# Attention scores on row quarters of the array, ACT and POOL in DVE's place, and a third buffer of expert products

## What is computed

```python
# 1: context-query attention (softmax over the context's tokens, then one linear layer of 4*128)
# 2: 8 experts, the best 2 weigh (weights from a softmax of two logits); all 8 are computed:
for e in range(8):
    u = x @ W1[e]; v = x @ W2[e]          # 128 -> 256
    y = (u * sigmoid(u) * v) @ W3[e]      # 256 -> 128
    out = out + y * weights[..., e]
# 3: cross attention, 16 heads of 8 features
scores = einsum('bqhd,bkhd->bhqk', Q, K) / sqrt(8)
attn = softmax(scores); out = einsum('bhqk,bkhd->bqhd', attn, V) @ W_o + b_o
# 4: x rounded to fp8, times an fp8 matrix, rescaled, plus bias
```

## Time and profile before

| | us |
|---|---|
| median of 3 runs | 224.56 (223.74 to 224.80) |
| the profiled execution | 223.94 |
| its span, first to last instruction | 222.0 |
| mean granted clock | 0.954 |
| experts (48 to 105) | 57.0 |
| change of stage (105 to 126.3) | 21.3 |
| batch 0 of the attention (126.3 to 147.2) | 20.9 |
| groups 4 to 11, nearly all in the loop (147.2 to 184.5) | 37.3 |
| groups 12 to 14 (184.5 to 197.6) | 13.1 |

### The profile page before, as it was taken

The page is one execution under the profiler, slowest core; times in us unless marked ns, Lnnn a source line. Parts: engine busy times, 40 slices in busy tenths (PEclk is TensorE's granted clock), DMA queues, the critical chain, the costliest instruction groups (busy, mean ns, idle before and its releaser), DMA issues.

```text
span 222.0 us, 4112 instructions
## 1 busy us (share of the span) xinstructions
PE 188.2 (85%) x1300; PEld 150.4 (68%) x1300; DVE 152.4 (69%) x431; ACT 118.1 (53%) x233; POOL 61.3 (28%) x88
## 2 busy tenths in 40 slices
PE   5698997999999999998799689789999999885130
PEld 4386796788778788887698577566777776653020
DVE  2899567655367446445557986798889899735754
ACT  2276586533222222523353369977988789574352
POOL 3725263960000000200220154322224222203602
PEclk9979999999999999999999889999999999999755
DMA  7999100000000000000000000000000000000002
GB/s 226 410 403 369 51 0 1 0 3 0 0 4 0 0 0 3 0 0 0 3 0 0 1 0 4 0 4 0 1 3 0 0 0 0 3 0 0 0 1 94
DMA packets 4225, 8.81 MB, mean 40 GB/s; under 512 B 880, under 2 KB 1904, under 8 KB 3952
## 3 DMA queue, kind: packets, MB, share of 16 engines
q1 hardware_dynamic: 2480, 7.60, 9.0%
q10 hardware_dynamic: 1728, 1.00, 1.5%
HBM read 5.98 MB, written 0.52 MB: 29 GB/s over the span
## 4 chain that ended last, share of the span: by engine, by line
PE 63%; DVE 18%; ACT 7%; issue 7%; POOL 2%; DMA 1%; DVEq 0%; ACTq 0%; POOLq 0%
PE banks L1181 11%; PE bank L1015 7%; PE banks L1231 7%; PE bank L1212 6%; PE bank L1016 6%; PE bank L1017 5%; PE bank L1243 5%; DVE attT L815 4%; DVE negm L872 2%; PE banks L1016 2%; PE banks L1015 2%; PE banks L1017 2%; PE bank L1220 2%; DVE stats L621 2%; ACT raw L504 2%
## 5 line engine op out<-in xcount | busy, mean ns | idle before, releaser
L872 DVE TENSOR_REDUCE negm<-bank 128x2 f32<-128x512 f32 x64 | 42.0, 686 | 4.5 <-PE bank L1212 3.0
L448 ACT ACTIVATE att<-bank 128x512 f32<-128x512 f32 x32 | 19.2, 599 | 41.5 <-PE bank L1017 28.7
L301 POOL TENSOR_TENSOR keyed<-rest,const 32x256 fp32r<-32x256 f32 x32 | 19.5, 610 | 65.2 <-DVE rest L862 58.0
L504 ACT ACTIVATE raw<-banks 128x1024 f32<-128x1024 f32 x32 | 32.5, 1022 | 2.8 <-PE banks L1231 2.4
L815 DVE TENSOR_TENSOR attT<-att,bank 128x512 f32<-128x512 f32 x16 | 11.0, 687 | 33.2 <-PE banks L1181 33.0
L1181 PEld LDWEIGHTS banks<-raw,attT 128*128 128x128 f32 x256 | 30.7, 192 | 1.7 <-issue 0.7
L1181 PE MATMUL banks<-raw,attT 128*128 128x128 f32 x256 | 31.2, 275 | 0.3 <-DVE xs L827 0.3
L1212 PE MATMUL bank<-keyed 128*128 128x512 f32 x64 | 25.0, 434 | 2.2 <-DVE keyed L882 1.3
L1015 PE MATMUL bank<-xT,w 128*128 128x512 f32 x48 | 20.9, 435 | 2.8 <-DVE xT L755 1.4
L1231 PE MATMUL banks<-keyed 128*128 128x256 f32 x128 | 19.1, 293 | 0.0
L1231 PEld LDWEIGHTS banks<-keyed 128*128 128x128 f32 x128 | 17.9, 196 | 1.6 <-issue 0.4
(11 more groups left out here) (199 smaller groups left out, 368.6 us busy)
## 6 DMA issues: line engine op xcount, KB each, us to landing
raw<-in_w SPq DMA_DIRECT2D x1, 2048.0 KB, 10.5
keyed<-negm SPq DMA_DIRECT2D x1, 2048.0 KB, 8.8
raw<-in_w SPq DMA_DIRECT2D x1, 1024.0 KB, 10.4
xs<-in_x SPq DMA_DIRECT2D x2, 256.0 KB, 3.4
ctxT<-in_ctxT SPq DMA_DIRECT2D x1, 512.0 KB, 4.5
ctx<-in_ctx SPq DMA_DIRECT2D x1, 512.0 KB, 5.5
wl<-in_wl SPq DMA_DIRECT2D x1, 256.0 KB, 5.8
wqkraw<-in_wq ACTq DMA_DIRECT2D x1, 256.0 KB, 9.3
```

The source lines that it names most:

```text
L301: pool.tensor_tensor(km[rows, g, j, :], ks[rows, g % 2, :], const[rows, C_ZERO:C_ZERO + 1].broadcast_to([QUAD, SEQ]), ALU.add)\
L448: act.activation(silus[:, k, :], bk[2 * k][:, :], ACT.Silu).then_inc(S["silu_s"], 1)
L504: act.activation(probs[:, g % 2, 2 * r:2 * r + 2, :, :].rearrange("p h k q -> p (h k q)"), pair[r][:, :], ACT.Exp, scale=ATT_SCALE).then_i ...
L872: dve.tensor_reduce(negm[:, g % 2, r // 2, c0:c0 + QUAD + 1:QUAD], bk[1 + r % 2][:, :].rearrange("p (h k) -> p h k", h=2), AX.X, ALU.max, ...
```

## The change

It has three parts.

**Row quarters.** The masked copies and the transfer that clears them are gone. A score matmul now names a row quarter (`tile_position=(32*r, 0)`) and takes only the 32 rows of one head, from the stacked terms themselves. A piece of `scores` is now one head with both halves of the tokens: two matmuls of 256 columns. `shifted_scores` is eight matmuls as before, but in the order of the quarters, first for one half of the keys and then for the other.

**The stacked terms.** ACT alone reads the projection's bank: two scaled and shifted roundings of 256 columns into `taken` and a copy of 512 columns into `whole`, in the place of its two roundings. POOL adds the two into `terms`, queries and keys at once, for group m+3 where it made the masks of m+2. DVE has no part in it. The projection of the next group waits for ACT's reading alone (split_s).

**Three product buffers.** `hid` has a third part, in the second half of `att`, and `hidden(n)` waits for down(n-3).

```diff
-        hid = attT[:, :, :, :].rearrange("p (n a) b c -> p n a (b c)", n=2)
+        hid = [attT[:, 0:2, :, :].rearrange("p a b c -> p a (b c)"), attT[:, 2:4, :, :].rearrange("p a b c -> p a (b c)"),
+               att_flat[:, TOK:2 * TOK].rearrange("p (k t) -> p k t", k=HB)]
...
-            blank = negm[:, :, :, :].rearrange("p u t c -> p (u t c)").unsqueeze(1).broadcast_to([P, 2 * G, HALF])
-            sp.dma_start(plain(keyed[:, 0:G * HPG * SEQ]).rearrange("p (n c) -> p n c", n=2 * G), blank)\
-                .then_inc(S["km_zero"], 16)
...
+            def stacked_terms(m, g, slot, first):
+                pool.wait_ge(S["split_s"], m + 1)
                 if not first:
+                    pool.wait_ge(S["qa_s"], m - 3)
                     pool.wait_ge(S["s2_ps"], 2 * (m - 3))
-                for j in range(2, HPG):
-                    rows = slice(QUAD * j, QUAD * (j + 1))
-                    pool.tensor_tensor(km[rows, g, j, :], ks[rows, g % 2, :],
-                                       const[rows, C_ZERO:C_ZERO + 1].broadcast_to([QUAD, SEQ]), ALU.add)\
-                        .then_inc(S["km_pool"], 1)
-                    pool.wait_ge(S["km_pool"], 2 * m + j - 1)
+                pool.tensor_tensor(terms[:, g, :, :].rearrange("p a c -> p (a c)"), whole[:, slot, :],
+                                   plain(taken[:, slot, :]), ALU.add).then_inc(S["stack_s"], 1)
...
+            def split(m, slot, first, bank=0):
                 act.wait_ge(S["proj_ps"], m + 1)
...
+                act.activation(taken[:, slot, 0:SEQ], bk[bank][:, 0:SEQ], ACT.Identity,
+                               scale=const[:, C_AQ:C_AQ + 1], bias=const[:, C_ZERO:C_ZERO + 1])
+                act.activation(taken[:, slot, SEQ:2 * SEQ], bk[bank][:, SEQ:2 * SEQ], ACT.Identity,
+                               scale=const[:, C_AK:C_AK + 1], bias=const[:, C_ONE:C_ONE + 1])
+                act.copy(whole[:, slot, :], bk[bank][:, :]).then_inc(S["split_s"], 1)
...
-                    if n > 1:
-                        dve.wait_ge(S["y_ps"], n - 1)
-                    dve.tensor_tensor(hid[:, p, k, :], silus[:, k, :], bk[2 * k + 1][:, :], ALU.mult)\
+                    if n > 2:
+                        dve.wait_ge(S["y_ps"], n - 2)
+                    dve.tensor_tensor(hid[n % 3][:, k, :], silus[:, k, :], bk[2 * k + 1][:, :], ALU.mult)\
...
-                pe.matmul(bk[1 + r % 2][:, :], qs[:, g, t * P:(t + 1) * P],
-                          km[:, g, 2 * pair:2 * pair + 2, :].rearrange("p h k -> p (h k)"),
-                          start=True, stop=True).then_inc(S["s1_ps"], 1)
+                rows = slice(QUAD * r, QUAD * (r + 1))
+                for t in range(TPB):
+                    ins = pe.matmul(bk[1 + r % 2][:, t * SEQ:(t + 1) * SEQ], qs[rows, g, t * P:(t + 1) * P],
+                                    ks[rows, g, :], start=True, stop=True, tile_position=(QUAD * r, 0))
+                ins.then_inc(S["s1_ps"], 1)
...
+                for t in range(TPB):
+                    for j in range(HPG):
+                        if not first and t == 0 and j % 2 == 0:
+                            pe.wait_ge(S["p_s"], 2 * (m - 1) + j // 2 + 1)
+                        rows = slice(QUAD * j, QUAD * (j + 1))
+                        ins = pe.matmul(bk[3 + j][:, t * SEQ:(t + 1) * SEQ], ks[rows, g, t * P:(t + 1) * P],
+                                        qa[rows, g, :], start=True, stop=True, tile_position=(QUAD * j, 0))
+                        if t == TPB - 1 and j % 2:
+                            ins.then_inc(S["s2_ps"], 1)
```

## The result

The changed kernel takes 233.0 us (231.7 to 236.1, 4 runs), the kernel before beside it 224.7; ratio 1.0356, interval 1.0297 to 1.0416: 8.3 us slower, where 1.9 faster was forecast, and outside the range. The profiled execution took 231.7 us, span 229.9. Medians are of all executions; the ratios, and the single times of e2, e3, e13 and e14, leave out executions more than 1.5% above the fastest of their kernel (no median given here moves by more than 0.5 us without them), among them the profiled ones of e2, e4, e11 and e14.

A forecast was written before the change was run, and what follows sets the result against it. After the change a cycle through ACT's exps and projection readings was to bound the loop. Experts and transition -5.8, batch 0 +0.6, loop +4.1, end -0.8 sum to -1.9: 222.4 us, range 215.5 to 227.8.

The forecast's parts named there:

- Third buffer: Expert stretch and change of stage: units of 4.5 us for 4.96, no wait on down products; -5.8 us in all.
- The cycle: Attention loop: second exp, shifted and third scores, projection, ACT's readings, next second exp; 4.9 us a group for 3.83.
- the exits: TensorE leaving row quarters for another array division, three more times in the cycle: 0.2 us each, 0.6 a group.
- no pause: Rival: changing between array divisions costs nothing in the loop; cycle 4.3 us, total 214 to 215; chance 0.26.
- no overlap: Rival: row-quarter score matmuls don't overlap, 0.48 us more a group, 228.1 us in all; chance 0.18.
- chores: Once a batch, ten TensorE records in the cycle (turned outputs, normalised, output layer): 1.1 us.
- With 1.3 idle of 4.9 it should hold: Loop: TensorE's clock stays full although it idles 1.3 us of each 4.9 us group.
- this rival: The clock falls to half; TensorE's 2.4 us of the cycle nearly double in all groups, 235 or more; chance 0.04.
- Batch 0: First four attention groups at 4.9 us each plus extras: 21.5 us for 20.9, +0.6.
- End: From group 12 on, only the first group has a projection: 12.3 us for 13.1, -0.8.
- The condition of failing as a whole: The forecast fails as a whole if the cycle through ACT isn't what the loop waits for.
- the best case of the forecast: Row-quarter scores run four at a time: eight shifted ones in two waves, 0.24 us for 0.95.

The follow-up runs named there:

- e2: Changed kernel plus a 512-column ACT copy into scratch per group, between the projection readings and the second exp: 246.9 us.
- e3: Changed kernel plus a 512-column ACT copy into scratch per group, ahead of the group's first exp: 233.6 us.
- e13: Changed kernel plus three filler matmuls per group in TensorE's wait for the second exp, in the loop and in batch 0: 225.7 and 225.8 us.
- e14: As e13, plus eleven filler matmuls between the last expert unit and group 0: 225.8 and 228.8 us.
- e4: Changed kernel with ACT's three readings of the projection moved behind the group's second exp: 223.2 us.
- e11: Changed kernel plus three filler matmuls per group in TensorE's wait for the second exp, in the loop only: 226.6 us.
- e7: Changed kernel with the first turned outputs of a batch moved behind the shifted scores: 232.8 us.
- e8: Changed kernel with the stacked terms made as before (two ACT readings, DVE's additions), keeping row quarters and third buffer: 222.6 us.
- e9: e8 with the first score piece of the next but one group placed beside the third piece: 222.6 us.
- e1: Kernel before with the third product buffer and nothing else: 217.8 us.
- e16: e8 plus filler matmuls: two ahead of the third score piece in most groups, eleven between experts and group 0: 227.9 us.
- e6: Changed kernel with the first score piece of the next but one group placed beside the third piece: 226.7 us.
- e5: Changed kernel plus four filler matmuls per group, between the outputs and the first two scores: 242.3 us.

## Why the prediction was wrong

**Third buffer, right.** 4.54 us a unit for the forecast 4.5; -5.8 forecast, -4.7 (profiled) to -6.9 (medians) measured. In the changed kernel group 0 came 4.8 us earlier, and the first projection 4.0, not 5.5. Counted from the first down products, which start 1.7 us later in that execution, it is 6.5 and 5.7 us: the gain is there, and the rest is how long the unchanged first block happened to take.

**The cycle, right in its path and nearly in its size.** At full clock the loop takes 42.2 us (e13) for the forecast 41.4. ACT's three readings take 1.38 (166.03 to 167.41) for 1.48, the exits show as 0.2 us before L953, L1146, L953, and the six shifted scores and third piece go in waves (begun at 163.28, they let the first exp start at 163.72). So neither "no pause" nor "no overlap" held. What was missed is the second group of a batch: forecast 5.35 (the mean 4.9 and chores), measured 6.1 to 6.2 at full clock, because its turned outputs wait for ACT's copy behind the late exp. The batch's other three are 0.3 us under their forecast together. I had put the turned outputs in the cycle by their length and not by what they wait for. e7 shows that moving them only changes what waits.

**"With 1.3 idle of 4.9 it should hold" is the step that failed.** I gave the clock a chance of 0.04 and thought of it as all groups or none. It fell in single stretches of 3.4 us, four of them behind batch 0, with TensorE idle 0.6 to 1.2 of 3.4 us before them; in the kernel before, at 98% busy, none. By e13 this costs 4.6 us in the loop and groups 12 to 14, by e11 6.4 over the kernel. The price named for this rival, 235 or more, was that of half clock throughout, and its own term, 2.4 us in each of 12 groups, would have given 29 us rather than 13. The clock is not the whole miss: with filler in the loop the changed kernel (226.6, e11) is still 4.2 us over the forecast.

**Batch 0, +3.2 where +0.6 was forecast.** Row quarters do most of it: e8 and e9, with VectorE's stacks, have the same 13.7 us at half clock and e8 +2.3, e1 has 3.4 us and none of the 2.3. Before, TensorE was busy all of the 3.4 us after the fall and the clock came back; in the changed kernel it was busy 3.21 of 3.40, then 9.19 of 10.30, and it came back only at 135.3. How the 3.2 us divide between clock and longer chain is open: no run had batch 0 at full clock, and where filler cut the time at half clock the stretch hardly changed (e13: 6.8 us at half, 23.7 in all; e16, on e8's 13.7 and 23.2: 10.2 and 24.0).

**End, +2.5 where -0.8 was forecast.** 2.4 of the 3.3 us are clock (e13); the remaining 0.9 are chain, not traced further.

In sum the miss, 9.9 us by the rounded figures of the table, is 1.0 ahead of group 0 (less than the late start of the profiled execution), 2.6 in batch 0, 3.0 in the loop (2.2 clock, 0.8 chain) and 3.3 behind it (2.4 clock, 0.9 chain). The condition of failing as a whole, that the loop waits for something else than the cycle through ACT, did not occur: e4, which takes the readings out of it, brings the loop from 44.4 to 38.8 us, for 42.2 by full clock alone.

## What to carry to other kernels

Where a change turns a TensorE-bound loop into one bound by a cycle through another engine, price the clock as a term of its own: here it fell now and then in a loop where TensorE, at full clock, idled 0.9 us a group (160.4 to 175.2), and held in e6's with 0.8 and e4's with 0.5. To tell cycle from clock, put a few filler matmuls inside the wait (not ahead of it: e5) and compare with the same groups at full clock. Count from the same instruction in both traces, as a late start moves everything behind it. And look at each thing that an in-order engine does once in several groups for what it waits for, not for its length.

## What the runs showed of the hardware

- TensorE's clock fell from 2.4 to 1.2 GHz after stretches in which it was busy 1.7 to 2.8 of 3.4 us. In loops in which it was 98 or 99% busy it did not fall; but it held too in e4's, busy 34.8 of 38.8 us, in e6's, 34.6 of 40.8, and in the kernel before through 1.93 of 3.40, so that busy time alone doesn't say when it falls.
- In the loop 6.8 us at half clock cost 2.2 us. By the Trainium skill ("TensorE: Matmul & The Clock Gate", HAM oscillation) time at half clock costs half of itself, by which I estimate 3.4 us here. The trace is below it; that TensorE waited for ACT in part of that time anyway is my reading of it.
- Row quarters overlap, also across instructions of different kinds. In the changed kernel a first-scores and a shifted-scores matmul start 0.01 us apart, and eight shifted ones take 0.51 us (above, 174.30), so that the best case of the forecast holds:

```profile
161.93 0.39 PE L1146 MATMUL bank<-terms 32*128 32x256 f32 x2
...
161.94 0.38 PE L1165 MATMUL banks<-qa,terms 32*128 32x256 f32 x1
```

- Entering or leaving row quarters showed 0.2 us each time (169.51 to 169.73, where projection matmuls start 0.12 apart; 169.73 to 170.16 for two quarter matmuls of 0.11 each), as column quarters do; taking two of them away gained nothing where TensorE waits for DVE's maximum in their place (e9).
